# Local attention in a hybrid network: the next batch normalised ahead of the exponential and turned right behind the scores

## The reference, cut to what matters

```
x = jnp.roll(x, -shift, axis=1)                      # shift = 16
qkv = xw @ w_qkv.T + b_qkv
sim = einsum('bwphd,bwqhd->bhwpq', q, k) * scale + rel_pos[...]
sim = where(mask, -inf, sim)                         # the last window only
probs = softmax(sim, axis=-1)
out = einsum('bhwpq,bwqhd->bwphd', probs, v) @ w_out.T + b_out
t = t + roll(out, shift, axis=1)                     # of layernorm(t)
```

## Time and profile before

| | us |
|---|---|
| Median of 3 runs | 1440.48 (1434.47 to 1440.89) |
| Profiled execution, its time | 1442.49 |
| Its span, first to last instruction | 1440.7 |
| TensorE busy | 1195.0 (83%) |
| VectorE busy | 917.4 (64%) |
| POOL busy | 589.5 (41%) |
| ScalarE busy | 562.0 (39%) |

### The profile page before, as it was taken

The page is one execution under the profiler, slowest core; times in us unless marked ns, Lnnn a source line. Parts: engine busy times, 40 slices in busy tenths (PEclk is TensorE's granted clock), DMA queues, the critical chain, the costliest instruction groups (busy, mean ns, idle before and its releaser), DMA issues. The chain is left out here.

```text
span 1440.7 us, 31184 instructions
## 1 busy us (share of the span) xinstructions
PE 1195.0 (83%) x11614; PEld 1031.0 (72%) x11614; DVE 917.4 (64%) x2231; ACT 562.0 (39%) x1293; POOL 589.5 (41%) x651
## 2 busy tenths in 40 slices
PE   7999998888483999999996674858489999999960
PEld 4555557677482999999993453635489999999960
DVE  4777775578661754466643776565538877788862
ACT  3444442146360655555554441533233323323310
POOL 5000002000336767756204771077200775567665
PEclk9999999899555999999997785769569999999985
DMA  8600000000402333434324110011012333334343
GB/s 318 284 0 1 0 1 8 1 1 1 140 23 67 116 124 120 129 112 123 96 63 164 52 40 2 1 50 54 20 30 67 109 118 105 100 113 116 104 133 105
DMA packets 87095, 115.66 MB, mean 80 GB/s; under 512 B 18371, under 2 KB 71142, under 8 KB 86694
## 3 DMA queue, kind: packets, MB, share of 16 engines
q1 hardware_dynamic: 65990, 62.92, 14.0%
q0 software_dynamic: 20960, 50.76, 10.8%
HBM read 53.19 MB, written 60.42 MB: 79 GB/s over the span
## 5 line engine op out<-in xcount | busy, mean ns | idle before, releaser
L1419 POOL DMA_INDIRECT sorted_rows<-s_normed,s_places x128 | 134.8, 1053 | 185.7 <-DVE s_places L1365 144.6
L1496 POOL DMA_INDIRECT gx_fetch<-sorted_results,g_places x128 | 131.7, 1029 | 125.7 <-DMA sorted_results<-gx_yq 66.5
L1496 POOL DMA_INDIRECT sx_fetch<-sorted_results,s_places x128 | 136.5, 1066 | 85.4 <-issue 33.5
L1579 PE MATMUL g_bank<-weights,gx_hT 128*128 x1360 | 165.8, 275 | 0.2 <-ACT gx_hT L1607 0.2
L1419 POOL DMA_INDIRECT sorted_rows<-g_normed,g_places x128 | 132.5, 1035 | 68.2 <-issue 36.0
L1579 PEld LDWEIGHTS g_bank<-weights,gx_hT 128*128 128x128 f32 x1360 | 158.4, 192 | 0.7 <-issue 0.7
L1542 PE MATMUL s_bank<-sx_xT_high,sx_w_now 128*128 128x256 f32 (+1 forms) x510 | 151.3, 297 | 1.8 <-DVE sx_hT L1654 1.2
L1544 PE MATMUL s_bank<-sx_xT_high,sx_w_now 128*128 128x256 f32 (+1 forms) x510 | 143.7, 282 | 0.0
L1543 PE MATMUL s_bank<-sx_xT_low,sx_w_now 128*128 128x256 f32 (+1 forms) x510 | 143.5, 281 | 0.0
L1607 ACT ACTIVATE gx_hT<-g_bank,gx_b_now 128x256 f32<-128x256 f32 x340 | 133.1, 482 | 3.0 <-PE g_bank L1579 3.0
L1579 PE MATMUL s_bank<-weights,sx_hT 128*128 (+1 forms) x1020 | 129.7, 276 | 2.9 <-DVE sx_yq L1665 1.4
(11 more groups left out here) (423 smaller groups left out, 2732.1 us busy)
## 6 DMA issues: line engine op xcount, KB each, us to landing
sorted_rows<-zeros POOLq DMA_DIRECT2D x29, 512.0 KB, 15.5
gx_xq<-sorted_rows SPq DMA_DIRECT2D x85, 128.0 KB, 2.1
sorted_results<-gx_yq SPq DMA_DIRECT2D x85, 128.0 KB
sx_xq<-sorted_rows SPq DMA_DIRECT2D x85, 128.0 KB, 2.1
sorted_results<-sx_yq SPq DMA_DIRECT2D x85, 128.0 KB
feats<-in_x SPq DMA_DIRECT2D x8, 512.0 KB, 7.3
out<-tokens SPq DMA_DIRECT2D x16, 256.0 KB, 3.9
s_raw<-in_silu_up SPq DMA_DIRECT2D x1, 2736.0 KB, 10.0
```

Of the source, the lines that this page charges most:

```text
L1419: pool.indirect_dma_start(out=sorted_rows[g], out_offset=bass.IndirectOffsetOnAxis(ap=places[:, at, r:r + 1], axis=0), in_=normed[:, at, : ...
L1496: pool.indirect_dma_start(out=fetch[n % 2][:, i, r, :], out_offset=None, in_=self.sorted_results[g], in_offset=bass.IndirectOffsetOnAxis(a ...
L1579: done = pe.matmul(down[u % 2][:, P * k:P * k + C], hT[u % 2][0:width, i, P * k:P * k + P], self.w_down[0:width, bass.ds(e, 1), i, :].rear ...
```

## The change

On TensorE the turn of the next batch moves from behind the mix to right behind the scores. On ScalarE the normalisation of the next batch moves from behind the exponential to ahead of it. Both are done in the step of (b, 0), if there is a next batch.

```diff
@@ WindowAttention.tensor, step(b, h)
                 scores(b, 0)
             elif b >= 1:
                 scores(b - 1, 1)
+            if h == 0 and b < self.n - 1:
+                turn_batch(b + 1)
             if h == 0 and b >= 2:
                 give(b - 2, 1)
             if b >= 1:
                 mix(b - 1, h)
-            if h == 0 and b < self.n - 1:
-                turn_batch(b + 1)
@@ WindowAttention.scalar, step(b, h)
         def step(b, h):
             take_qk(b, h)
+            if h == 0 and b < self.n - 1:
+                normalise(b + 1)
             if h == 1:
                 exponent(b, 0)
             elif b >= 1:
                 exponent(b - 1, 1)
-            if h == 0 and b < self.n - 1:
-                normalise(b + 1)
             if b >= 1:
                 take_mixed(b - 1, h)
```

## The result

| | before | after |
|---|---|---|
| Median, us (18 runs each, one comparison) | 1442.44 | 1432.85 |
| Ratio after / before, 95% interval | | 0.9944 (0.9932 to 0.9956) |
| Profiled execution, us (its span) | 1442.49 (1440.7) | 1436.42 (1434.7) |
| First part: from VectorE's L749 for the part's batches 2 and 3 to its last addition L2189, starts | 799.38 to 888.49: 89.11 | 798.67 to 887.79: 89.12 |
| Second part: from VectorE's first L749 of the part to its last L2189, starts | 894.67 to 1032.84: 138.17 | 893.98 to 1026.22: 132.24 |

The change makes the kernel 8.1 us faster by the ratio (6.3 to 9.8). The two medians lie 9.6 us apart; gains are given by the ratio throughout. One of the runs before was slow, 1516.34 us, and is not in the ratio. In the profiled pair the span falls by 6.0 us: 5.9 of it in the second part, nothing in the first.

A forecast was written before the change was run, and what follows sets the result against it. It took the chain of exponential, normalisation, turn, projection, scores and softmax in the window attention as the bound. Gains of 1.3 + 3.4 + 3.6 = 8.3 us off the median 1440.48 gave 1432.2, range 1427.5 to 1438 (8 in 10).

The forecast's parts named there:

- What bounds it: Window attention, 23rd to 31st slices: chain of exponential, normalisation, turn, projection, scores, softmax; VectorE stands 6.25 us for a projection.
- Change to batch 2, second part: Batches 4 to 7: normalisation right behind k, then turn and mix; projection ends 3.4 us earlier, bounds 2.0 and 3.8.
- Change to batch 3: Second part: turn waits 0.2 us instead of 2.60, projection ends 3.6 us earlier, bounds 1.9 and 4.4.
- The rest of the second part: Behind the two changes: TensorE-bound expert units and a gather tail follow, so the gains reach the end whole.
- rival 4: Behind the turn: clock stays at 0.50 through the next half batch; 7 us slower, or 1447; chance 0.05.
- First part: Batches 0 to 3: VectorE's last eight additions alternate with POOL's weight splitting, so only 1.3 us reach the end.
- Rival 1: Second part, both changes: projection stays at the low clock behind the mix; gain 5.2 us, or 1435.3; chance 0.18.
- rival 2: First part keeps its gain, its additions taking 2.68 us: 10 us in place of 1.3, about 1424; chance 0.05.
- rival 3: At the changes the turn is not what is late and another wait takes over whole: 1440.5; chance 0.07.

The follow-up runs named there:

- e3: Changed kernel with TensorE's turn put back behind the mix, leaving ScalarE's move alone; ratio to the kernel before 0.9915 (-12.3 us).
- e2: Kernel before with both moves made in the first part (batches 0 to 3) only; ratio to the kernel before 0.9984 (-2.3 us).
- e5: Kernel before plus one wait: POOL splits weights (L2413) only after VectorE's last gather addition; ratio to the kernel before 0.9976 (-3.5 us).
- e6: Changed kernel plus one wait: POOL splits weights (L2413) only after VectorE's last gather addition; ratio to the kernel before 0.9900 (-14.4 us).
- e1: Kernel before with both moves made in the second part (batches 4 to 7) only; ratio to the kernel before 0.9950 (-7.2 us).
- e4: Changed kernel with ScalarE's normalisation put back behind the exponential, leaving TensorE's move alone; ratio to the kernel before 1.0065 (+9.4 us).
- e8: The changed kernel, unaltered, timed again; ratio to the kernel before 0.9936 (-9.2 us).
- e11: Repeat of e6, the changed kernel with POOL's late splitting; ratio to the kernel before 0.9892 (-15.6 us).

## Why the prediction was right, and where it was not

The forecast of 1432.2 us and the gain of 8.3 came true in size: 8.1 us (6.3 to 9.8), median 1432.85. That the two figures lie so close is in part luck. In the profiled pair the two parts together give 5.9 us, not 8.3, and the 2 us between that and the ratio are not assigned. Averaged over the profiles with the same code, the second part falls by 6.9 (137.3 to 130.4), where the forecast has 7.0, and the first by 0.0 to 1.6, where it has 1.3. By its steps:

- **What bounds it.** Right, though the slices that fall are the 22nd to the 30th, not the 23rd to the 31st. The chain of exponential, normalisation, turn, projection was the one that set the end, and e3 shows which link mattered: taking the normalisation out from behind the exponential brings the whole gain.
- **Change to batch 2, second part: 3.4 us.** Measured 3.1. The pieces agree: normalisation 3.18, turn at 951.07, mix without idle time, projection 3.46 where I took 3.2, as the clock was still at 0.50 when it began and reached 1.00 only at 956.5. The exponential, moved behind the table load, came 0.04 us later relative to k (4.38 after its end, 4.34 before), as nearly nothing as forecast.
- **Change to batch 3: 3.6 us.** Measured 3.75, and here too the agreement is partly luck. The turn's wait went and the clock was high (1.09 us), as forecast. But from the end of k to the end of the scores it took 4.14 us (968.56 to 972.70) where the sum has 3.00, because the rest of the projection ahead and the start of the give were at the low clock. The stop of 0.76 that the sum kept in the mix was absent, which nearly made up for it.
- **The rest of the second part: no loss.** Nearly. 3.1 + 3.75 = 6.8 at the two places, 5.9 at the end: 0.3 is lost between them and 0.5 behind the second. The 0.3 belongs to the projection at 964.05 that took 5.49 us at the low clock, 1.1 more than before; the rest of its delay lies in the 4.14 above. That the clock is low through later work resembles rival 4, at a sixth of its price, but the clock had been high through the scores and fell behind them, where the rival had it low from the turn on.
- **First part: 1.3 us.** Measured 0.0 and 0.2 in the change's profiles, 1.6 in e2 and e3. The mechanism was right: VectorE came 5.5 us earlier, the eight additions alternated with POOL's splittings, and e5 and e6 show it by taking the splitting away, which uncovers 2.8 us. Two terms were off. POOL's gathers were to end 0.46 us earlier by its wait for VectorE; that wait went, but they ended 0.78 later (855.32, not 854.54), since a stop among them that the profile doesn't explain took 2.21 us (1.68 before) and some gathers took longer. This term alone decides between 0.0 and 1.6 (above, at e1 and e2). And the last gather landed at 856.94, a wait for a transfer of 2.44 us that I did not have; what it cost in the change isn't shown.
- **The rivals.** Rival 1 fell with the projections of 3.46 and 2.84 us, rival 2 with the 11.06 us of the last additions, rival 3 with the 5.9 us of the second part. Rival 4 asks for a clock still at 0.50 when the scores start; in their stretch it was 0.93.
- **What the prediction did not ask.** It took the two moves as one. Its own sum had the price of TensorE's move in it ("The mix, now behind it, takes 2.06"), and set beside TensorE's wait for the normalisation it shows that more than half of the mix fits into the wait if it stays ahead. Only e3 and e4 brought that out: the gain is ScalarE's move, 12.3 us, and TensorE's is a cost, alone or in the pair.

## What to carry to other kernels

When a change moves several steps, sum each move by itself before summing them together: here the one is worth more than the pair. Work whose inputs are ready belongs ahead of an instruction that will wait, not behind it. And a gain in front of work that another engine slows as long as it runs is largely swallowed there; look whether that engine's work can be moved out of the way (here 3.5 us, and 5.2 with the change).

## What the runs showed of the hardware

Beside POOL's L2413 only some of VectorE's instructions are slowed: with both inputs in SBUF, L1704 (0.34 us alone, 1.4 in the changed kernel's last group, 11.06 / 8), L2179 (0.69 to 2.03) and L2171 (0.69 to 1.32). L2167, which has one input in the bank, and L2170 and L2183, which have a single input, keep their 0.65, 0.69 and 0.71 us. The Trainium skill, "SBUF — State Buffer", section "Who interferes with whom", states just that division (two SBUF inputs contend with a GpSimd instruction that reads SBUF; at most one, outside certain fast modes, does not), and these rows agree. POOL's eight L2413 take 12.09 us beside eight additions in the changed kernel, 12.90 beside some five in the kernel before and 12.71 beside the softmax in e5; no run shows them alone.

A projection of the same shape took from 2.8 to 5.5 us in these profiles. The one at 964.05 stood wholly at the 0.50 level in the change, in e8 and e11 (5.49 each), and partly so in e1 and e6 (4.30 and 4.36), with the same code in the second part. That is 1.2 of the 5 us by which profiles of that code differ; what decides it isn't shown.
